# Issuing the output stores of the last stage from SyncE's queue instead of ScalarE's, with the next input load ahead of each

## The reference

```python
U_plus = jnp.fft.irfft(Vf[None, :, :, None] * Uf_p[:, :, None, :], n=n, axis=1)[:, :sl]
...
out = jnp.einsum('btkd,k,kde->bte', U_plus, s, Mpp)
out = out + jnp.einsum('btkd,k,kde->bte', U_minus, s, Mpm)
...
t = t + _L1_ffn_ref(_ln_t(t), ...)      # weights one-hot over the four lengths
x = _from_tokens(t, x)                  # the output
```

## Time and profile before

| | before |
|---|---|
| median of three runs | 1830.44 us |
| the profiled execution | 1828.1 us |
| its span | 1826.8 us |
| granted TensorE clock, mean | 0.978 |
| PE busy | 1730.3 us (95%) |
| DVE busy | 1313.4 us (72%) |
| ACT busy | 1198.5 us (66%) |
| SP queue (q1) | 170.45 MB |
| ACT queue (q10) | 6.02 MB |

### The profile page before, as it was taken

How to read it: one execution, slowest core, us unless ns; L and a number is a source line. 1 busy time by engine, 2 the same in 40 slices (tenths; PEclk the granted TensorE clock), 3 DMA queues, 4 the chain that set the end, 5 groups by cost and what they waited for, 6 DMA issues and landing times.

```text
span 1826.8 us, 76477 instructions
## 1 busy us (share of the span) xinstructions
PE 1730.3 (95%) x32475; PEld 1388.1 (76%) x32475; DVE 1313.4 (72%) x3787; ACT 1198.5 (66%) x2619; POOL 638.0 (35%) x815
## 2 busy tenths in 40 slices
PE   5899999999999998989999999999999999998998
PEld 3566676666767665888788888888888888876776
DVE  2677778888867766795677777777777777656775
ACT  5788888888877654646677777777777777640000
POOL 6544455556545534030533122333322333100000
PEclk8899999999999988999999999999999999999999
DMA  4422333433233323387322122212212221369852
GB/s 118 114 80 76 105 85 93 109 84 102 72 91 96 85 66 93 120 266 236 98 60 58 49 54 68 69 47 69 57 36 68 68 68 48 78 185 255 249 150 71
DMA packets 266001, 182.52 MB, mean 100 GB/s; under 512 B 39888, under 2 KB 263022, under 8 KB 263966
## 3 DMA queue, kind: packets, MB, share of 16 engines
q1 hardware_dynamic: 257098, 170.45, 34.1%
q10 hardware_dynamic: 7924, 6.02, 1.1%
q0 software_dynamic: 640, 1.16, 0.2%
HBM read 107.03 MB, written 70.63 MB: 97 GB/s over the span
## 4 chain that ended last, share of the span: by engine, by line
PE 73%; DVE 12%; issue 5%; POOL 4%; ACT 4%; DMA 1%; SPq 1%; DVEq 0%; POOLq 0%; ACTq 0%
PE banks L1401 21%; PE banks L1379 10%; PE banks L1382 9%; PE banks L1601 8%; PE banks L409 5%; DVE zone L610 4%; PE banks L403 3%; PE banks L368 2%; PE banks L358 2%; PE banks L416 2%; PE banks L382 2%; DVE st L597 1%; PE banks L456 1%; PE banks L322 1%; DVE W L652 1%
## 5 line engine op out<-in xcount | busy, mean ns | idle before, releaser
L1434 DVE COPY Gm<-banks 128x448 f32<-128x448 f32 x896 | 552.9, 639 | 209.6 <-PE banks L1379 126.8
L1420 ACT ACTIVATE Gm<-banks 128x448 f32<-128x448 f32 x896 | 514.7, 628 | 198.6 <-PE banks L1379 149.8
L1401 PE MATMUL banks<-Gm,U 128*32 128x128 f32 x12544 | 517.7, 275 | 10.9 <-issue 7.5
L1401 PEld LDWEIGHTS banks<-Gm,U 128*32 128x32 f32 x12544 | 339.3, 110 | 54.5 <-issue 50.9
L1382 PE MATMUL banks<-V,zone 118*32 118x224 bf16 x7040 | 294.4, 260 | 0.4 <-issue 0.4
L1379 PE MATMUL banks<-V,zone 118*128 118x224 bf16 x1824 | 215.6, 261 | 0.7 <-ACT qT L1206 0.5
L872 POOL TENSOR_TENSOR W<-W,mx 128x280 f32<-128x280 f32 x196 | 130.6, 666 | 226.5 <-DVE mx L659 225.1
L1382 PEld LDWEIGHTS banks<-V,zone 118*32 118x32 bf16 x7040 | 195.0, 97 | 1.7 <-issue 1.3
L1379 PEld LDWEIGHTS banks<-V,zone 118*128 118x128 bf16 x1824 | 157.3, 98 | 47.4 <-issue 39.1
L1601 PE MATMUL banks<-YC,zone 98*98 98x256 f32 x768 | 171.1, 383 | 3.3 <-DVE YC L1682 3.3
L1601 PEld LDWEIGHTS banks<-YC,zone 98*98 98x98 f32 x768 | 128.1, 167 | 50.1 <-issue 7.6
(11 more groups left out here) (174 smaller groups left out, 2676.4 us busy)
## 6 DMA issues: line engine op xcount, KB each, us to landing
Yd<-YS SPq DMA_DIRECT2D x112, 224.0 KB, 4.3
W<-Vd SPq DMA_DIRECT2D x392, 49.0 KB
zone<-Yd SPq DMA_DIRECT2D x32, 392.0 KB
YL<-Yd SPq DMA_DIRECT2D x32, 392.0 KB
UL<-Ud SPq DMA_DIRECT2D x27, 448.0 KB, 4.0
zone<-Mbf SPq DMA_DIRECT2D x28, 256.0 KB
Vd<-W SPq DMA_DIRECT2D x56, 112.0 KB
T<-XR SPq DMA_DIRECT2D x28, 224.0 KB, 2.5
```

Source lines behind the costliest of these rows:

```text
L1401: ins = e.matmul(p[32 * x:32 * x + 32, :], self.U7[(2 * P + ch) % 3][:, sl, 8 * (3 - q):8 * (3 - q) + 32], self.Gm[:, par, r:r + 2, :], st ...
L1420: e.activation(dst, src, ACT.Copy).then_inc(S["gm_act"], 1)
L1434: v.tensor_copy(dst, src).then_inc(S["gm_dve"], 1)
```

## The change

The stores of rounds 0 to 6 leave ScalarE's stream and are issued by SP, one at the end of each of SP's rounds. rn is issued one round earlier in SP's program: rn(n + 1) instead of rn(n), behind y(n + 2). The last store keeps its three pieces.

```diff
@@ scalar
             e.activation(self.PB[t % 2][:, :], self.bank("two", t), ACT.Copy).then_inc(S["half"], 1)
-            if t % 2 and t >= 3:
-                n = t // 2 - 1
-                e.wait_ge(S["kept"], 4 * n + 4)
-                e.wait_ge(S["turned"], 4 * n + 4)
-                self.store_rows(e, n, slice(0, 4))
@@ sync
-            if n:
-                if n >= 2:
-                    e.wait_ge(S[f"d_o{n % 2}"], 32 * ((n - 2) // 2 + 1))
-                load_out(e, D, S, n)
-        for name, count, rows in (("turned", 30, slice(0, 4, 3)), ("kept", 32, slice(1, 2)), ("turned", 32, slice(2, 3))):
-            e.wait_ge(S["kept"], 30)
-            e.wait_ge(S[name], count)
-            self.store_rows(e, 7, rows)
+            if n + 1 < 8:
+                if n >= 1:
+                    e.wait_ge(S[f"d_o{(n + 1) % 2}"], 32 * ((n - 1) // 2 + 1))
+                load_out(e, D, S, n + 1)
+            for name, count, rows in ((("turned", 4 * n + 4, slice(0, 4)),) if n < 7 else
+                                      (("turned", 30, slice(0, 4, 3)), ("kept", 32, slice(1, 2)), ("turned", 32, slice(2, 3)))):
+                e.wait_ge(S["kept"], 4 * n + 4 if n < 7 else 30)
+                e.wait_ge(S[name], count)
+                for k in range(2):
+                    e.dma_start(out_rows(self.out, n, k)[:, rows], self.RN[n % 2][:, k, rows]).then_inc(S[f"d_o{n % 2}"], 16)
```

More of the change, by code:

```diff
@@ L1651, in scalar @@
             e.activation(self.PB[t % 2][:, :], self.bank("two", t), ACT.Copy).then_inc(S["half"], 1)
-            if t % 2 and t >= 3:
-                n = t // 2 - 1
-                e.wait_ge(S["kept"], 4 * n + 4)
-                e.wait_ge(S["turned"], 4 * n + 4)
-                self.store_rows(e, n, slice(0, 4))
-    def store_rows(self, e, n, rows):
-        for k in range(2):
-            e.dma_start(out_rows(self.out, n, k)[:, rows], self.RN[n % 2][:, k, rows]).then_inc(self.S[f"d_o{n % 2}"], 16)
     def combine(self, v, n, h, k, a0=0, a1=4):
```

## The result

| | before | changed |
|---|---|---|
| median, 10 runs each | 1829.57 us | 1839.88 us |
| lowest to highest | 1826.66 to 1835.46 | 1836.31 to 1846.86 |
| profiled execution, its span | 1828.1, 1826.8 us | 1836.57, 1835.3 us |

The ratio is 1.0058, interval 1.004 to 1.0076: slower by 7 to 14 us. The forecast was 1831.2 us, range 1828.3 to 1837.5, so the time lies above the range, near rival B's 1840.3: TensorE waits at the turn in every second step.

What follows compares the result with a forecast made beforehand. TensorE was taken to bound the last stage. A gain of 1.46 us and a loss of 2.2 us from late y loads summed to +0.8 us, giving 1831.2 us on the median; range 1828.3 to 1837.5 us.

Steps and rivals of the forecast that it cites:

- rival B: Store-to-y ring bounds the last stage, TensorE waiting every second step from y(4): 1837.3 to 1840.3 us; chance 0.24.
- TensorE sets the end, and the removed wait is worth 1.46 us: Last stage: TensorE steps take 11.22 us; removing VectorE's 7.46 us wait on rn(1) gains only 1.46 us.
- ScalarE without stores gives nothing: Last stage: fourteen store issues leave ScalarE's stream beside 167.8 us idle behind TensorE; counted 0.
- The ring and its break-even at 17.47 us: Store, y, combine, line 1708, next store take l + 4.97 us; TensorE's two steps 22.44; loss above l = 17.47.
- l: Time from a store's release to the landing of the y queued behind it; five rounds lose 5 l - 87.63 us.
- Part 4: How long y takes behind a store on SP's queue: 16.8 us for two rounds, 18.7 for three; loss +2.2 us.
- part 1: rn(1) issued behind y(2) instead of y(3): VectorE's wait at line 1729 goes, -1.46 us; later rn cost nothing.
- Clock: TensorE's granted clock stays up with stalls of about 1 us; nothing added, though a 3 us stall might cost as much again.
- Range: Whole time from 1828.3, a little under rival A (only the gain stays, chance 0.27), to 1837.5 us, l = 19.2.
- the bound of 20.4: Upper bound of l, with y at 213 GB/s and the full 1.2 us tail: a loss of 14.4 us.
- The rule on issuing engines: All issuers share 16 DMA engines, so store and y go as fast as before; only the 1.46 us gain would show.

Runs made afterwards that it cites:

- e1: Changed kernel, all stores still on SP, but each y issued once its buffer is free, ahead of the store it stood behind; 0.9968 of before.
- e4: Changed kernel with the same wait on SP, but y(n + 3) issued before store(n) instead of behind it; 0.9984 of before.
- e2: Kernel before the change with only rn(1) moved ahead of y(3), stores left on ScalarE; 0.9983 of before.
- f1: Changed kernel run again without edits, for a second set of landing times; 1.0054 of before.
- g1: Changed kernel, but from round 1 on SP issues rn(n + 1) only when y(n + 2) has landed; 1.0018 of before.
- f2: Changed kernel with store(0) to store(6) writing one row group of four, three quarters of those rows left out; 0.9993 of before.
- f3: Changed kernel with store(0) to store(6) each written twice, the second copy to a scratch tensor; 1.014 of before.
- e3: Changed kernel with its waits kept on SP, but the stores issued by ScalarE as before the change; 0.9985 of before.
- g2: e1 repeated in another batch, on another chip; 1.0003 of before.
- g3: e2 repeated in another batch; 0.9992 of before.
- g4: Repeat: stores on SP, rn(n + 2) then y(n + 4) behind store(n), most of y(1) combined before y(0)'s last part; 0.9966 of before, median 1828.29 us.

## Why the prediction was wrong

- *TensorE sets the end, and the removed wait is worth 1.46 us*: right within S. Steps of 11.22 us, and S = 144.14 to 144.21 wherever y is in time (e1 to e4).
- *ScalarE without stores gives nothing*: right. e2, with the stores still on ScalarE, is as fast.
- *The ring and its break-even at 17.47 us*: right. The rule was a net of 5 l - 87.63 - 1.46 against before. With measured means of l it gives 7.3 us for f1 (S says 7.5), 3.3 for g1 (3.6), -1.46 for f2 (-1.1), and 25.1 for f3 (28.6, of which 3.3 are the step of 14.51 us behind the last stall, whose turn took 2.00 us instead of 1.02). In the changed kernel's first trace the four measured l have a mean of 19.34, 7.6 us (6.75). The agreement of f1 is partly luck: one of the five losses was the clock's.
- *Part 4, l = 16.8 us in the first two rounds and 18.7 in the last three*: **the step that failed**. Measured are 18.5 and 20.3 in the first two, and 19.1 to 19.5 in the others; f1 says 19.27 throughout, where the forecast's mean was 17.94. The ring turns each us of l into 5 us of time, so 1.3 us more make 6.7 us more. Of the 1.3 us, 0.8 are rn(n + 1), which part 1 cost at nothing because it stands behind y: I counted 4.01 MB as all that moves before y lands, but when rn is held back until y has landed, l falls by 0.8 us (g1). The other 0.5 us lie in the first two rounds: in g1 the last three l are 18.4 to 18.8, as forecast, and the first two 18.90 and 17.71, where 16.8 was forecast. I gave these rounds 265 GB/s, read from a stretch where one long backlog was being worked off; with store and y the stretch from 1684 to 1702 in f1 has 243 GB/s, while e4, without a store ahead, has 265 from 1680 to 1690. Why the rate is lower no run shows; it differs between rounds of one trace. The tail was also read a little short: from 1767.2 + 3.17 = 1770.4 to 1771.84 are 1.5 us, not 1.2, and half of it adds 0.1 us to l.

```profile
1684.00:1702.00 18.00, 16.12 (x72) 11.42 (x71) 10.54 (x18) 1.19 (x2) 0.00 (x0) 1.00 0.93 243
```
```profile
1680.00:1690.00 10.00, 10.00 (x46) 7.31 (x45) 5.88 (x11) 0.60 (x1) 0.00 (x0) 1.00 0.97 265
```

- *Clock*: I added nothing, expecting stalls of about 1 us. One of 2.58 us lowered it, and the step behind it took 3.07 us more. Part of that is not an extra: the longer step gave y(5) time, and that round had no wait.
- *Range*: its upper end, 1837.5, stood for l = 19.2, although the bound of 20.4 was worked out (a net of +12.9 us, 1843.4). With a term that the ring multiplies by five, the range had to reach nearer to that bound.
- *The rule on issuing engines* (the Trainium skill, "DMA: Bandwidth & Descriptors", "Issuing engines are not separate DMA queues"): e3 and e4 agree with it in time, 0.9985 with two queues and 0.9984 with one. They agree in rate too, which settles what I left open in part 4. e3 has 322 GB/s from 1684 to 1690, with loads and stores from two queues; e1 and e4, with all of them in SP's queue, reach 333 GB/s, and in e1 that queue moved nearly all of it (e1's stretch, its queue as packets, MB and share of the 16 engines, and e4's stretch):

```profile
1688.00:1690.00 2.00, 2.00 (x11) 1.53 (x10) 0.89 (x2) 0.00 (x0) 0.00 (x0) 1.00 0.96 333
```
```profile
q1 hardware_dynamic: 665, 0.66, 94.7%
```
```profile
1758.00:1760.00 2.00, 2.00 (x11) 1.54 (x10) 1.93 (x4) 0.38 (x1) 0.00 (x0) 1.00 0.95 333
```

So the high rate does not need the second queue. In the changed kernel, where the store goes ahead of y, no stretch of two us from 1674 to 1800 had more than 284 in the first trace.

What stays open: the median moved by 10.3 us, S by 6.8 and 7.5 in two traces. The rest lies ahead of S. From y(0)'s last combine to the last turn are 1822.11 - 1649.57 = 172.54 us before, 1830.59 - 1649.86 = 180.73 and 1840.88 - 1658.29 = 182.59 in the two traces of the changed kernel: 8.2 and 10.1 us more. y(2) is waited for longer, 0.43 us before, 1.46 and 2.63 after, and the third turn then waits for DF. The first two rows are of before, the others of f1:

```profile
1649.57 0.76 DVE L1678 TENSOR_TENSOR YC<-zone 98x256 f32<-98x256 f32 x2 [15.47 <-DMA zone<-Yd]
...
1666.98 1.22 DVE L1678 TENSOR_TENSOR YC<-zone 98x1024 f32<-98x1024 f32 x1 [0.43 <-DMA zone<-Yd]
```
```profile
1658.29 0.76 DVE L1669 TENSOR_TENSOR YC<-zone 98x256 f32<-98x256 f32 x2 [18.62 <-DMA zone<-Yd]
...
1678.39 1.23 DVE L1669 TENSOR_TENSOR YC<-zone 98x1024 f32<-98x1024 f32 x1 [2.63 <-DMA zone<-Yd]
```

From y(0)'s last combine to the third turn are 26.9 us before, 28.3 and 29.4 in the changed kernel, and 27.9 to 30.2 in e1 to e4, f2, g2 and g3, which all issue rn(1) right behind y(2). So moving rn(1) may cost here what it gains in S: e2 and g3, with rn(1) alone moved, have 172.15 and 174.37 us over the whole stretch, against 172.54. That rn(1) is the cause is not shown, as there is one trace of before.

## What to carry to other kernels

Where a load is queued behind a store that waits for the computation, look for the ring: store, load, use, next store. Compare its length with the period of the engine that bounds the kernel. A loss there comes once per round, so the landing time must be taken with everything that stands in the queue before and behind the load. Issue transfers in the order in which their conditions come true (e1), or at least the load first (e4); moving the issue to another engine was not what mattered.

## What the runs showed of the hardware

- Transfers behind a load in the same queue delay it: without rn behind y, l fell from 19.27 to 18.47 us (f1 and g1, means of five; the changed kernel's other trace has 18.5 to 20.3).
- The higher rate does not depend on two queues: 322 to 337 GB/s with loads in one queue and stores in the other (e3, before), 333 to 336 in two us with both in SP's queue (e1 from 1688 to 1690 and 1706 to 1708, e4 from 1758 to 1760). The three stretches of y alone in the earlier trace rows after 1700 have 213 to 255.
- TensorE's clock fell to the 1.2 GHz level after idle times of 2.58 us, once after 1.73 (f1, at 1784.41: granted 0.51 and 0.63 in the next two stretches) and once after 1.56 (g4), but stayed at 1.00 after 1.88 (f1, at 1687.70) and 1.30 (before). The idle time alone does not tell.

```profile
1786.00:1788.00 2.00, 2.00 (x6) 1.30 (x5) 1.77 (x4) 0.00 (x0) 0.00 (x0) 0.51 0.90 248
1788.00:1790.00 2.00, 2.00 (x7) 1.44 (x6) 0.00 (x0) 0.00 (x0) 0.00 (x0) 0.63 0.96 251
```
